# Recommendation tower on one core: feature products of two samples at a time on halves of the array, in four fills per tile instead of one sample at a time on quarters, in two

## The reference

```
e = stack([tbl_f[ids[:, f]] for f in range(26)], axis=1)      # 2048 x 26 x 128
combined = concatenate([e, r_dense_x[:, None, :]], axis=1)    # 27 rows a sample
interact = einsum('bfd,bgd->bfg', combined, combined)         # 27 x 27 a sample
z = interact[:, triu_i, triu_j]                               # 351 pairs
h = relu(concatenate([z, r_dense_x], 1) @ W_top1 + b_top1)    # 512
h = relu(h @ W_top2 + b_top2)                                 # 256
y = h @ W_top3                                                # 1
```

## Time and profile before

| | |
|---|---|
| median of 3 runs | 408.25 us (407.98 to 411.75) |
| profiled execution | 403.16 us, its span from the first to the last instruction 401.4 us |
| PE busy | 360.7 us (90% of the span), 6418 matmuls and as many weight loads |
| DVE, ACT, POOL busy | 223.7, 169.4, 259.0 us |
| mean granted clock of TensorE | 0.979 |

### The profile page before, as it was taken

The page is one execution under the profiler, slowest core; times in us unless marked ns, Lnnn a source line. Parts: engine busy times, 40 slices in busy tenths (PEclk is TensorE's granted clock), DMA queues, the critical chain, the costliest instruction groups (busy, mean ns, idle before and its releaser), DMA issues.

```text
span 401.4 us, 14335 instructions
## 1 busy us (share of the span) xinstructions
PE 360.7 (90%) x6418; PEld 330.1 (82%) x6418; DVE 223.7 (56%) x247; ACT 169.4 (42%) x473; POOL 259.0 (65%) x278
## 2 busy tenths in 40 slices
PE   3887979898989789997999989996999999998987
PEld 2676869797979689896989889895989989897766
DVE  4786699754466524574458735673356744651122
ACT  2444226254526235362544444361444535364522
POOL 6677777777777777777777777777774777710000
PEclk9998999999999969999999999997899999999999
DMA  6777543322233223222323222312221323200000
GB/s 175 233 220 221 161 114 89 87 80 58 65 82 70 60 54 93 59 80 54 80 68 82 79 57 65 85 51 77 54 76 54 80 56 93 58 16 3 3 2 2
DMA packets 17935, 32.03 MB, mean 80 GB/s; under 512 B 5737, under 2 KB 8689, under 8 KB 17873
## 3 DMA queue, kind: packets, MB, share of 16 engines
q0 software_dynamic: 8640, 17.71, 17.5%
q1 hardware_dynamic: 8352, 12.60, 10.5%
q10 hardware_dynamic: 880, 0.80, 0.6%
HBM read 31.08 MB, written 0.01 MB: 77 GB/s over the span
## 4 chain that ended last, share of the span: by engine, by line
PE 75%; DVE 8%; DMA 8%; issue 7%; ACT 1%; SPq 0%; DVEq 0%; ACTq 0%
PE x_ps L611 31%; PE tail_ps L684 16%; PE gram_ps L630 12%; PE x_ps L592 8%; DMA hot_in<-in_tbl 8%; DVE onehot L872 7%; PE tail_ps L661 2%; PE tail_ps L653 2%; PE tail_ps L690 2%; DVE hot_lo L858 1%; PE x_ps L721 1%; PE tail_ps L732 0%; DVE zt_lo L466 0%; PE x_ps L715 0%; PE x_ps L716 0%
## 5 line engine op out<-in xcount | busy, mean ns | idle before, releaser
L575 POOL DMA_INDIRECT raw<-in_tbl,ids_sb x270 | 258.1, 956 | 92.7 <-issue 78.9
L872 DVE TENSOR_TENSOR onehot<-ids_wide,row_ps 128x1024 fp32r<-128x1024 int16 (+1 forms) x163 | 183.9, 1161 | 88.3 <-PE x_ps L611 85.4
L611 PE MATMUL x_ps<-onehot,hot_hi 128*128 128x256 f32 x566 | 148.3, 297 | 7.1 <-issue 4.0
L611 PE MATMUL x_ps<-onehot,hot_lo 128*128 128x256 f32 x566 | 141.6, 284 | 0.0
L611 PEld LDWEIGHTS x_ps<-onehot,hot_hi 128*128 128x128 f32 x566 | 108.2, 191 | 11.9 <-issue 5.6
L611 PEld LDWEIGHTS x_ps<-onehot,hot_lo 128*128 128x128 f32 x566 | 108.5, 192 | 1.6 <-issue 1.6
L630 PE MATMUL gram_ps<-xt 128*27 128x26 f32 x4096 | 53.0, 193 | 21.5 <-issue 18.2
L388 ACT COPY xt<-x_ps 128x128 f32<-128x128 f32 (+1 forms) x100 | 45.6, 514 | 61.8 <-PE x_ps L611 61.0
L630 PEld LDWEIGHTS gram_ps<-xt 128*27 128x27 f32 x4096 | 44.1, 105 | 30.5 <-issue 24.5
L410 ACT COPY gram<-gram_ps 128x416 f32<-128x416 f32 (+1 forms) x32 | 16.2, 506 | 68.3 <-PE gram_ps L630 68.3
L819 ACT COPY xt<-x_ps 128x384 f32<-128x384 f32 (+1 forms) x78 | 44.5, 631 | 1.3 <-PE x_ps L592 1.3
(11 more groups left out here) (76 smaller groups left out, 315.6 us busy)
## 6 DMA issues: line engine op xcount, KB each, us to landing
ids_wide<-in_hot_ids SPq DMA_DIRECT2D x18, 256.0 KB
raw<-in_tbl,ids_sb POOLq DMA_INDIRECT x270, 3.0
hot_in<-in_tbl SPq DMA_DIRECT2D x14, 256.0 KB, 3.5
hot_in<-in_tbl SPq DMA_DIRECT2D x6, 320.0 KB, 3.9
weights_in_place<-in_w SPq DMA_DIRECT2D x10, 128.0 KB, 2.8
dense_sb<-in_dense_t ACTq DMA_DIRECT2D x6, 128.0 KB, 2.4
dense_sb<-in_dense_t SPq DMA_DIRECT2D x2, 128.0 KB, 3.6
w1d_sb<-in_w SPq DMA_DIRECT2D x2, 128.0 KB
```

Of the source, the lines that this page charges most:

```text
L575: nc.gpsimd.indirect_dma_start(out=raw[k][:, f, :], out_offset=None, in_=sources[f], in_offset=bass.IndirectOffsetOnAxis(ap=ids_sb[:, t, f ...
L611: last = nc.tensor.matmul(ps, table[:, chunk_at[j] + c, :], moving[:, c - a, :], start=(c == 0 and table is tables_of[0]), stop=(c == chun ...
L872: nc.vector.tensor_tensor(columns(p), ids_wide[:, it // IDS % IDS_RING, it % IDS, 0:width].unsqueeze(1).to_broadcast([P, n, width]), row_n ...
```

## The change

The products are formed for two samples at once. The weights are the 59 columns of two neighbouring samples (32 slots of the first, 27 of the second), the moving operand is 2 x 26 columns, and the result has 59 partitions by 52 columns, of which the two blocks on the diagonal are wanted. `LANES` = 2 such results stand on the two halves of the array. A bank now holds 8 groups of four samples, so a tile has `FILLS` = 4 fills of 16 matmuls (of two passes). `gram_copy` takes four instructions for a fill, one for each 32 partitions, since the wanted columns differ. The pad slots 27 to 31 of `xt` are cleared at the start by DVE, and ACT's first copy waits for that.

In `gram_slots` two fills make one step of the order. In the first tile of a block, the second hot item of the next block now goes between the two pairs of fills, and both items are held until after the second pair. The transposes zt 0 and zt 1 are issued at zt 0's place, alternating between the two tail banks.

```diff
-FILLS = 2
+LANES = 2
+FILLS = 4
@@ gram_slots
-        return [[("gram", t * n_gram + i)] + [step for slot in hot[cut[i]:cut[i + 1]] for step in slot] for i in range(n_gram)]
+        return [[("gram", t * n_gram + i + k) for k in range(2)] + [step for slot in hot[cut[i]:cut[i + 2]] for step in slot]
+                for i in range(0, n_gram, 2)]
@@ order of the slots
-            held = item_end[pieces[hot[0][0][1]][0]] - hot[0][0][1]
-            slots += hot[:held] + gram_slots(t)
-            slots[-1].append(("held", pieces[hot[0][0][1]][0]))
+            p, it = hot[0][0][1], pieces[hot[0][0][1]][0]
+            held = item_end[it + 1] - p
+            fills_of = gram_slots(t)
+            slots += hot[:item_end[it] - p] + fills_of[:1] + hot[item_end[it] - p:held] + fills_of[1:]
+            slots[-1] += [("held", it), ("held", it + 1)]
@@ gram_copy
-            copy(gram[rows, :, per_fill * i:per_fill * (i + 1)], src).then_inc(done, 1)
+            for s in quads:
+                rows, at = slice(SLOTS * s, SLOTS * (s + 1)), s % lane * (feats - 1)
+                last = copy(gram[rows, :, per_fill * i:per_fill * (i + 1)], src[rows, at:at + feats - 1, :])
+            last.then_inc(done, 1)
@@ products
-                    for s in range(QUAD):
+                    for s in range(0, QUAD, lane):
                         b = t % XT * P + (i * per_fill + g) * QUAD + s
-                        last = nc.tensor.matmul(gram_ps[m % 2][SLOTS * s:SLOTS * s + feats, cols],
-                                                xt[:, b, 0:feats], xt[:, b, 0:feats - 1], start=True, stop=True)
+                        last = nc.tensor.matmul(gram_ps[m % 2][SLOTS * s:SLOTS * s + lane_rows, cols],
+                                                xt[:, b:b + lane, :].rearrange("p b f -> p (b f)")[:, 0:lane_rows],
+                                                xt[:, b:b + lane, 0:feats - 1], start=True, stop=True)
@@ tail_step, zt 0 and 1
+            blocks_of = [z_blocks[0][0], z_blocks[1][0]] if j == 0 else [z_blocks[j][part]]
             for s in range(QUAD):
+                for bank_of, (odd, of) in zip((ps, tail_ps[tail_bank["zt", 1]]), blocks_of):
@@ vector
+            nc.vector.memset(xt[:, :, feats:], 0.0).then_inc(xt_cleared, 1)
```

More of the change, by code:

```diff
@@ L88, in build @@
     n_gram = FILLS
-    assert per_fill * (feats - 1) <= BANK
+    lane = QUAD // LANES
+    lane_rows, lane_cols = (lane - 1) * SLOTS + feats, lane * (feats - 1)
+    assert per_fill * lane_cols <= BANK
     gram_block = tiles_block * n_gram
@@ L349, in build @@
         hot_split = sem("hot_split")
+        xt_cleared = sem("xt_cleared")
         row_no_ready = sem("row_no_ready")
@@ L407, in gram_copy @@
                 reach(eng, tail_full["cols"], h * n_cols)
-            rows = slice(SLOTS * quads[0], SLOTS * (quads[-1] + 1))
-            src = gram_ps[m % 2][rows, 0:per_fill * (feats - 1)].rearrange("p (g c) -> p c g", g=per_fill)
-            copy(gram[rows, :, per_fill * i:per_fill * (i + 1)], src).then_inc(done, 1)
+            src = gram_ps[m % 2][:, 0:per_fill * lane_cols].rearrange("p (g c) -> p c g", g=per_fill)
+            for s in quads:
+                rows, at = slice(SLOTS * s, SLOTS * (s + 1)), s % lane * (feats - 1)
+                last = copy(gram[rows, :, per_fill * i:per_fill * (i + 1)], src[rows, at:at + feats - 1, :])
+            last.then_inc(done, 1)
         def product_copied(eng, m):
@@ L626, in products @@
                 for g in range(per_fill):
-                    cols = slice(g * (feats - 1), (g + 1) * (feats - 1))
-                    for s in range(QUAD):
+                    cols = slice(g * lane_cols, (g + 1) * lane_cols)
+                    for s in range(0, QUAD, lane):
                         b = t % XT * P + (i * per_fill + g) * QUAD + s
-                        last = nc.tensor.matmul(gram_ps[m % 2][SLOTS * s:SLOTS * s + feats, cols],
-                                                xt[:, b, 0:feats], xt[:, b, 0:feats - 1], start=True, stop=True)
+                        last = nc.tensor.matmul(gram_ps[m % 2][SLOTS * s:SLOTS * s + lane_rows, cols],
+                                                xt[:, b:b + lane, :].rearrange("p b f -> p (b f)")[:, 0:lane_rows],
+                                                xt[:, b:b + lane, 0:feats - 1], start=True, stop=True)
                 last.then_inc(gram_full, 1)
@@ L643, in tail_step @@
                 ps = tail_ps[bank]
+                if key == ("zt", 1):
+                    return
                 if part == 0:
@@ L655, in tail_step @@
                 elif kind == "zt":
-                    odd, of = z_blocks[j][part]
                     if part > 0:
                         pe.wait_ge(rest_turned, h + 1)
-                    rows = slice(odd * groups_block, (odd + 1) * groups_block)
+                    if j == 0:
+                        other = tail_bank["zt", 1]
+                        reach(pe, tail_copied[other], h * tail_per[other] + tail_nth["zt", 1])
+                    blocks_of = [z_blocks[0][0], z_blocks[1][0]] if j == 0 else [z_blocks[j][part]]
                     for s in range(QUAD):
-                        last = nc.tensor.transpose(
-                            ps[0:of.stop - of.start, s * groups_block:(s + 1) * groups_block],
-                            z[rows, s, of], ident[rows, rows])
+                        for bank_of, (odd, of) in zip((ps, tail_ps[tail_bank["zt", 1]]), blocks_of):
+                            rows = slice(odd * groups_block, (odd + 1) * groups_block)
+                            last = nc.tensor.transpose(
+                                bank_of[0:of.stop - of.start, s * groups_block:(s + 1) * groups_block],
+                                z[rows, s, of], ident[rows, rows])
+                            if s == QUAD - 1 and j == 0 and odd == 0:
+                                last.then_inc(tail_full[kind], 1)
                     if part < parts[key] - 1:
@@ L789, in hot_copy @@
                 act.wait_ge(piece_used, item_end[it])
+                if it == 0:
+                    act.wait_ge(xt_cleared, 1)
                 to_xt(copy, first, n, nf + j, x_ps[fill_no["hot", it] % len(x_ps)]).then_inc(x_copied, 1)
```

## The result

The changed kernel takes 410.2 us (median of 20 executions, 407.7 to 412.9), the kernel before 407.7 us on the same chips (401.6 to 413.2): a ratio of 1.012, 95% interval 1.009 to 1.016. The forecast was 394, in a range of 385 to 404. It was wrong in size and in sign: the kernel became 1.2% slower where a gain of 3.5% was forecast.

What follows compares the result with a forecast made beforehand. PE, with stops for instruction fetch, was taken to bound the kernel. From 403.2 us: - 15.1 (products) + 7.5 (new wait) - 3.4 (clock) = 392.2; with half a half-clock stretch allowed, 394 us, range 385 to 404.

Steps and rivals of the forecast that it cites:

- What bounds the kernel: Whole kernel: PE, busy 90% of the span, sets the time; its long stops are instructions fetched too slowly.
- Part 1: Product matmuls on PE: 2048 passes of 26.7 ns and no long stops, 76.4 to 60.8 us, 15.6 us gained.
- my 76.4: Product matmuls before the change: 74.5 us busy and idle, plus a 1.9 us stop behind a fill.
- Part 2: ACT's product copies: 0.225 us apart, so PE newly waits 1.25 us in blocks 1 to 6, 7.5 us lost.
- The sign that I had named for copies too far apart: Product fills on PE: waits of L639 for ACT would show copies longer than 0.33 us apart.
- Part 3: TensorE's clock: one of two 6.8 us half-clock stretches goes with the stops, 3.4 us gained, between 0 and 6.8.
- my rule of half a stretch: PE work at clock 0.50: half speed costs half the stretch, 3.4 us of 6.8.
- Part 4: Alternating transposes 0 (-0.3 to +0.2 us a block), pad clearing 1.8 us hidden, last copies at most 0.2 later, POOL off path.
- The sum: Whole kernel: 403.2 - 15.1 + 7.5 - 3.4 = 392.2 us, forecast as 394 us.
- ACT becomes what PE waits for: ACT's copies at 0.33 us, waits in some second tiles too: 13 to 18 us lost, 400 to 405; chance 0.10.
- My rival on the slower side: Product matmuls: loads and streams in series on a half, a pass of 46 ns, 435 us; chance 0.05.

Runs made afterwards that it cites:

- The last run: Each product matmul issued twice into the same place, against the kernel with one held item: 440.3 us (one execution).

## Why the prediction was wrong, point by point

**What bounds the kernel: right.** PE, and the stops as instructions that come late. The last run shows the pace to be the condition.

**Part 1, the products: right in kind, 3.3 us too large.** The pass of 26.7 ns measured 27.3, over 128 passes in the last run 27.5, and the pair of 1.90 us 1.94. The Trainium skill's rule (TensorE: Matmul & The Clock Gate, section Packing small matmuls), by which load and stream would have stood in series at 46 ns, isn't borne out here: the rows show 27.3. The group is 62.4 + 1.7 = 64.1 us where I said 60.8: 1.6 for the passes and their ends, 0.7 for new waits, and 1.0 is the last tile's wait for ACT's copy, which stood in my 76.4 and could not go. The gain was 12.3, not 15.6. The fetch packets came to 35, under 40, as I said.

**Part 2, ACT's copies: the spacing mis-sized, and the wait with it.** I put the copies 0.225 us apart, between rows in which copies overlap, with 0.33 as the high end "(no overlap)". They stand 0.335 apart. By my own count with that value the wait is 2.1 us a block; it measured 2.05, 12.3 us in all against 7.5, at the high end of 13. The wait also costs 0.4 us more than it shows, since the turns' part grew by 2.4. The place, the number and the releaser were right. The sign that I had named for copies too far apart, waits of L639 for ACT's product copies, was the wrong place to look: those are 0.5 us. ACT's load was too small as well, by a slip (1.06 x 4 is 4.2, not 3.6) and by the overlap: ACT is busy 232.7 us where I said near 210. What I didn't see is that the wait isn't the bank's alone: the h1 stage stands second in the same queue.

**Part 3, the clock: this step failed.** I wrote that one of the two long stretches would go, 3.4 us gained, and that "The new waits of 1.25 us are shorter than the stops, but they might keep one alive", and gave that no price. Both old stretches went, which by my rule of half a stretch is 6.8 us gained. But the waits, 2.05 us in every block, brought six stretches of their own, about 1.5 us each, 9.2 us together as the run in which PE works through the wait shows. So the clock cost some 2.4 us net where I had a gain of 3.4. I took the clock for a rider on the stops that were removed and did not price it for the wait that was added.

Behind that stood a misreading. I had the clock fall "each time after PE had two stops in one tile". The kernel before shows it otherwise (PE, then windows with the granted clock third from the end):

```profile
138.46 0.38 PE L661 MATMUL tail_ps<-ident,z 64*64 64x64 f32 x4 [1.93 <-issue]
138.77 1.87 PE L630 MATMUL gram_ps<-xt 128*27 128x26 f32 x124
142.18 0.30 PE L630 MATMUL gram_ps<-xt 128*27 128x26 f32 x4 [1.54 <-issue]
```

```profile
138.46:139.90 1.44, 1.39 (x105) 1.21 (x106) 0.42 (x1) 0.37 (x1) 0.94 (x1) 1.00 0.25 57
139.90:142.10 2.20, 0.74 (x44) 0.50 (x34) 0.00 (x0) 0.00 (x0) 1.65 (x2) 0.50 0.25 58
```

The clock fell at 139.9, behind the first stop and before the second had ended; near 276 it fell at 276.5, right behind a stop that ended at 276.3, and the second ended at 280.3. One halt of 1.76 to 1.93 us was enough, so a single new wait of that length had to be priced. It was no rule either: six stops of 1.69 to 1.98 us stood in front of products and transposes in blocks 2 to 7, and four of them, the one of 1.98 us in tile 6 among them, were followed by no fall. What decides it beside the length stays open; no run tried it.

**Part 4: right.** Alternation 0 (44.2 us a block either way). The clearing of the pads took 1.66 us and ended at 4.07 us, ahead of the 5.2 that I had named; PE started at 7.24 us against 6.99, held by a DMA and not by DVE. POOL did not come onto the path.

**The sum.** Block by block, from 401.4 us: - 4.9 in the first two tiles, + 3.3, - 1.3, + 2.7, + 3.2, - 0.3, + 4.2 in blocks 1 to 6, each as the kernel before had stops and half clock there or not, - 0.5 after them: 407.8. By the terms of my sum, 392.2 against the 409.7 of the profiled execution: 3.3 us are the products, 7.2 the wait (4.8 as PE shows it and 2.4 beside it in the turns), and 5.8 the clock by my rule of half a stretch; about 1 us is left. The product part by itself is a gain: with one held item the kernel takes 393.5 us, 16.6 less than with two. The second held item buys what PE waits between the fills of one tile, 0.7 us a block, and costs 4.2.

**The rivals.** The nearest was "ACT becomes what PE waits for", 400 to 405, with 0.10. Its price left out the clock; with 9 us for that it would have reached the result. My rival on the slower side asked for a slow pass and was the wrong one. All cases with a new wait should have carried the clock's price with them, and the range, which ended at 404 for want of it, would have held the time.

## What to carry to other kernels

A wait on the engine that sets the time has two prices: its length, and the half-speed work behind it where the clock falls; look in the trace at what followed each halt of about the same length, to the instruction, and add that, as a range where the halts differ, to every wait that a change brings. When a copy is split into four that do a quarter of the rows each, allow for four times the time (here 324 ns a quarter against 332 ns for the whole), and look at who stands behind them in that engine's queue: all of them, since moving the first one out of the way here only let the second one wait. To part what an edit consists of (here the products, the second held item, the alternation), run each alone; the sum hid a gain of 2.4% (ratio 0.976) under a loss of 3.7% (1.012 over 0.976).

## What the runs showed of the hardware

- A copy of 32 x 208 from `gram_ps` on ACT starts 335 ns behind the one before it and takes 324; one of 128 x 208 takes 332. On DVE the 32 x 208 copy takes 376. Other copies of this kernel on ACT overlap by 0.11 us; these don't. Why not stays open, it wasn't tried.
- TensorE's clock went to 0.50 for 3.4 us behind waits of 2.05 to 2.2 us in 16 blocks of 18 (the changed kernel twice, and the run with the held copy first), behind waits of 1.7 us in three blocks of six, behind two of the six stops of 1.69 to 1.98 us in blocks 2 to 7 of the kernel before, and not behind the waits of 1.6 us in block 1 with one held item (two runs) or of 0.9 us in the runs that share the copies. It did not where PE repeated transposes in that time. The length alone doesn't decide it.
- 59 x 52 products on array halves run at 27.5 ns a pass over 128 of them, with no stop for instructions at 4096 passes. 27 x 26 products on quarters at 8.5 to 15 ns a pass came to 18.2 us of such stops at as many passes.
- Free of stops, the one-sample products would take 4.4 us for a block of 256 samples (an estimate from 8.5 ns a pass), the two-sample products take 7.0 (256 at 27.3); the larger form wins only by what it asks of the supply of instructions.
